# A twelve-stage decoder on one core: the delta-rule stage without its loop, and another order of work in the selective-scan stage

## The reference, cut to what matters

```
hs, gate = split(x @ Win.T)                       # 512 channels each
hs = silu(causal_conv4(hs) + bconv)
dt_in, Bm, Cm = split(hs @ Wx.T)                  # 128, 16, 16
dt = softplus(dt_in @ Wdt.T + bdt)
dA = exp(A * dt);  dBu = dt * Bm * hs             # per channel and state n of 16
h_t = dA_t * h_(t-1) + dBu_t;  y_t = sum_n h_t * C_t
out = ((y + hs * D) * silu(gate)) @ Wout.T
```

```
q, k, v = split(silu(causal_conv4(x @ Wqkv.T)));  z = x @ Wz.T
beta = sigmoid(x @ Wb.T);  g = -exp(A_log) * softplus(x @ Wa.T + dt_bias)
state = exp(g_t) * state
state = state + k_t (v_t - state k_t) * beta_t;   out_t = state q_t
result = (rmsnorm(out) * norm_w * silu(z)) @ Wout.T
```

## Time and profile before

| | |
|---|---|
| profiled execution | 4954.54 us |
| its span, first to last instruction | 4952.8 us |
| median of three runs | 4951.31 us |
| PE busy | 4182.5 us (84%) |
| DVE busy | 3232.5 us (65%) |
| ACT busy | 2130.0 us (43%) |
| POOL busy | 1507.2 us (30%) |
| scans of l2_attn | from 977.05 to 1516.1 us |
| steps of l3_attn | from 2326.7 to 4287.2 us |
| mean granted PE clock, share of full speed | 0.926 |
| instruction queues q8 and q14 | 464 packets, 7.60 MB; 127 packets, 1.04 MB |

### The profile page before, as it was taken

One profiled execution on the slowest core, in us unless ns is written; L12 is line 12 of the kernel. 1 busy time (PEld: TensorE's weight loads), 2 busy tenths in 40 slices (PEclk: granted clock), 3 DMA queues, 4 the chain that ended last, 5 costly groups with the idle time before them and its releaser, 6 DMA issues. The chain is left out here.

```text
span 4952.8 us, 145582 instructions
## 1 busy us (share of the span) xinstructions
PE 4182.5 (84%) x62052; PEld 2732.9 (55%) x62052; DVE 3232.5 (65%) x6011; ACT 2130.0 (43%) x3774; POOL 1507.2 (30%) x1609
## 2 busy tenths in 40 slices
PE   7626886677767887997999999999999999779999
PEld 6515654323324664444676767676766767545555
DVE  6797644688887777744677777777777777531111
ACT  3446443644444554323554555555555555321111
POOL 1001100188893220000343433333433333212222
PEclk9869887888899998998999999999999999789999
DMA  0000000133341001001000000000000000031111
GB/s 32 18 26 10 0 12 19 46 116 114 123 141 45 1 1 33 20 0 39 18 20 21 20 21 20 21 20 21 21 23 21 20 20 4 8 115 49 53 54 45
DMA packets 70627, 174.60 MB, mean 35 GB/s; under 512 B 14322, under 2 KB 27636, under 8 KB 67444
## 3 DMA queue, kind: packets, MB, share of 16 engines
q1 hardware_dynamic: 70036, 165.96, 10.6%
HBM read 163.04 MB, written 2.88 MB: 34 GB/s over the span
## 5 line engine op out<-in xcount | busy, mean ns | idle before, releaser
L2416 POOL TENSOR_TENSOR dn_eb<-dn_ee,dn_cc 128x512 f32<-128x512 f32 x64 | 66.7, 1042 | 1119.6 <-DVE dn_cc L2530 1119.6
L2956 DVE TENSOR_TENSOR moe_hh<-moe_si,moe_pu 128x512 f32<-128x512 f32 x104 | 71.5, 688 | 450.5 <-PE moe_pu L2845 444.2
L1667 POOL TENSOR_TENSOR ssm_ub<-ssm_dtu,ssm_bcn 128x512 f32<-128x512 f32 x256 | 319.6, 1269 | 31.9 <-DVE ssm_ph L1726 29.1
L2123 PE MATMUL dn_bA<-core_XT,dn_w 128*128 128x512 f32 x512 | 274.3, 661 | 59.6 <-issue 41.3
L2460 DVE SCALAR_TENSOR_TENSOR core_XN<-dn_bA,dn_w,core_XN 128x504 f32<-128x504 f32 (+2 forms) x384 | 280.8, 731 | 44.0 <-ACT core_XN L2297 24.0
L1628 ACT ACTIVATE ssm_da<-core_XN,ssm_al 128x504 f32<-128x504 f32 x256 | 173.9, 683 | 253.5 <-DVE ssm_ph L1726 156.6
L1565 PE MATMUL ssm_py<-ssm_hc,core_ident 128*128 128x512 f32 x352 | 201.7, 675 | 74.6 <-DVE ssm_hc L1730 44.4
L2908 POOL TENSOR_TENSOR moe_hw<-moe_hh,moe_cb 128x512 f32<-128x512 f32 x100 | 126.7, 1267 | 451.5 <-DVE moe_hh L2956 392.3
L2889 ACT ACTIVATE moe_si<-moe_pg 128x512 f32<-128x512 f32 x104 | 62.1, 597 | 466.1 <-PE moe_pg L2845 466.1
L1726 DVE TENSOR_TENSOR_SCAN ssm_ph<-ssm_da,ssm_ub 128x512 f32<-128x512 f32 x176 | 214.7, 1220 | 47.6 <-ACT ssm_da L1628 25.5
L2255 PE MATMUL dn_po<-dn_wo,dn_cT 128*128 128x256 f32 x1024 | 240.8, 389 | 1.1 <-ACT dn_cT L2357 1.1
(11 more groups left out here) (515 smaller groups left out, 10511.3 us busy)
## 6 DMA issues: line engine op xcount, KB each, us to landing
ssm_bcn<-ssm_bct SPq DMA_DIRECT2D x128, 512.0 KB, 3.6
dn_cb<-dn_cum SPq DMA_DIRECT2D x32, 512.0 KB, 8.0
dn_w<-in_dn_w SPq DMA_DIRECT2D x16, 776.0 KB, 4.9
moe_cb<-moe_rows SPq DMA_DIRECT2D x64, 192.0 KB, 2.8
moe_w<-in_moe_w SPq DMA_DIRECT2D x26, 384.0 KB, 9.9
moe_cb<-moe_rows SPq DMA_DIRECT2D x64, 128.0 KB, 3.0
dn_wo<-in_dn_w SPq DMA_DIRECT2D x16, 256.0 KB, 3.7
moe_cb<-moe_rows SPq DMA_DIRECT2D x64, 64.0 KB, 2.6
```

The lines of the kernel that those rows point to most:

```text
L1667: pool.tensor_tensor(ub[u % NUB][:, :], dtu[q % 2][:, c, :], bcn[i % NB][:, 0, :], ALU.mult).then_inc(ub_ready, 1)
L2123: mm = pe.matmul(bank[:, :], wp[:, kc, gi * P:(gi + 1) * P], g.XT[:, kc, q * CH:(q + 1) * CH], start=kc == 0, stop=kc == DC - 1)
```

## The change

In l3_attn the loops go. `schedule` now writes out all 66 steps for each engine, and SP's loads are written out for all 16 heads. All waits are for the running sum from the start of the stage; `settle` and `take_now`, which took the counts off again, are gone. Addresses that were worked out from the loop's counter become constants. The order of the instructions of each engine is the same as before.

In l2_attn the order is another. Four decay factors (units 20 to 23 of each chunk) are computed into a new SBUF tile `dx` ahead of silu in the job S, so the scans of these units read `dx` in place of `da`. The gate projections Z of chunk 0 and the D jobs 2 and 3 are not ahead of the first unit: the Z stand between units 3 and 12 (as "Y"). D 0 now comes before X 1. The dt and dtu of D 0 and D 1 are made by VectorE. TensorE's X waits for each silu block alone. `ub` has four slots in place of three, `hc` four in place of eight.

```diff
-    NB, NUB, NHC = 4, 3, 8
+    NB, NUB, NHC, NDX = 4, 4, 4, 4
+        dx = s.sb("dx", [P, NDX, CH])
...
-        ahead = [("H", 0), ("H", 1), ("H", 2), ("H", 3), ("S", 0), ("X", 0), ("X", 1), ("D", 0), ("D", 1), ("D", 2), ("D", 3),
-                 ("Z", 0), ("Z", 1), ("Z", 2), ("Z", 3)]
+        ahead = [("H", 0), ("H", 1), ("H", 2), ("H", 3), ("S", 0), ("X", 0), ("D", 0), ("X", 1), ("D", 1)]
+        AT.update({("Y", c): 3 + 3 * c for c in range(IC)})
...
+            if j[0] == "Y":
+                return None if q else (0, ("Z", j[1]))
...
+        silu_at = AT["S", 0]
+        apart = lambda u: 0 <= u % (IC * N) - silu_at < NDX
+        factor = lambda u: dx[:, u % (IC * N) - silu_at, :] if apart(u) else da[:, u % 2, :]
...
                     elif kind == "X":
-                        pe.wait_ge(hs_ready, IC * (q + 1))
                         for kc in range(IC):
+                            pe.wait_ge(hs_ready, IC * q + kc + 1)
...
+                def decay(u):
+                    k, n, cc = split(u)
+                    q, c = k // 2, k % 2 * 2 + cc
+                    act.activation(nb(factor(u))[:, :, 1:S], nb(dt[q % 2][:, c, :])[:, :, 1:S], ACT.Exp,
+                                   scale=al[:, n, c:c + 1]).then_inc(da_ready, 1)
...
                     elif kind == "S":
+                        if q:
+                            for n in range(NDX):
+                                decay((q - 1) * IC * N + silu_at + n)
                         act.preload_act_table_set("silu_and_others")
...
+                    if apart(u):
+                        return
                     if u >= 2:
-                        act.wait_ge(scan_done, u - 1)
+                        act.wait_ge(scan_done, u - 1 - (NDX if apart(u - 2) else 0))
+                    decay(u)
...
-                    if kind == "D":
+                    if kind == "D" and q * IC + c >= 2:
                         pool.wait_ge(sp_ready, q * IC + c + 1)
...
                         dve.tensor_scalar(mm0[:, c % 2, :], out, tap(K + 2, c), 0.0, ALU.add, ALU.max).then_inc(m_ready, 1)
+                        if q * IC + c < 2:
+                            dve.wait_ge(sp_ready, c + 1)
+                            dve.drain()
+                            dve.tensor_tensor(dt[q][:, c, :], mm0[:, c, :], sa[:, c, :], ALU.add).then_inc(dt_ready, 1)
+                            dve.drain()
+                            dve.tensor_tensor(dtu[q][:, c, :], dt[q][:, c, :], hs[q][:, c, :], ALU.mult).then_inc(dtu_ready, 1)
...
-                        dve.tensor_tensor_scan(ph[:, m % 2, :], da[:, u % 2, :], ub[u % NUB][:, :], 0.0, ALU.mult, ALU.add).then_inc(scan_done, 1)
+                        dve.tensor_tensor_scan(ph[:, m % 2, :], factor(u), ub[u % NUB][:, :], 0.0, ALU.mult, ALU.add).then_inc(scan_done, 1)
...
-        def schedule(eng, step):
-
-            step(0, 0)
-            step(1, 0)
-            settle(eng)
-            with eng.Fori(0, 7) as a8:
-                for k in range(8):
-                    step(k + 2, a8 * 2)
-                settle(eng)
-            for i in range(58, NSTEP + 2):
-                step(i, 0)
-            settle(eng)
+        def schedule(step):
+
+            for i in range(NSTEP + 2):
+                step(i)
...
-                with nc.sync.Fori(1, NKH // 2) as kh2:
-                    for u in range(2):
-                        row = a["dn_w"][bass.ds(kh2 * 2 + u, 1), :, :]
-                        load_w(u, row)
-                        load_cb(u, kh2 * 2 + u)
-                        load_wo(u, row)
+                for kh in range(NKH):
+                    row = a["dn_w"][kh:kh + 1, :, :]
+                    if kh:
+                        load_w(kh % 2, row)
+                    load_cb(kh % 2, kh)
+                    load_wo(kh % 2, row)
```

More of the change, by code:

```diff
@@ L1447, in jobs_at @@
                 return q + 1, j
-        order = [(0, j) for j in ahead if j[0] != "S" and j not in later.values()]
+        order = [(0, j) for j in ahead if j[0] != "S"]
         for q in range(NQ):
@@ L1476, in schedule @@
             for j in ahead:
-                if j not in later.values():
-                    job(0, j)
+                job(0, j)
             for u in range(NU):
@@ L1662, in unit @@
                     q, c, i = k // 2, k % 2 * 2 + cc, u // 2
+                    if u < 2:
+                        pool.wait_ge(dtu_ready, u + 1)
                     if cc == 0:
@@ L1681, in _ @@
                     dve.memset(nb(da[:, k, :])[:, :, 0:1], 0.0)
+                for k in range(NDX):
+                    dve.memset(nb(dx[:, k, :])[:, :, 0:1], 0.0)
                 dve.drain().then_inc(a_exp, 1)
@@ L2182, in level_x, with step @@
                     mm.then_inc(px_ready, 1)
-                def step(i, _):
+                def step(i):
                     new, mid, old = i < NSTEP, 0 < i <= NSTEP, i >= 2
@@ L2278, in _ @@
                 pe.matmul(bB[:, :], lt[:, :], gg[:, :, :].rearrange("p t h -> p (t h)"), start=True, stop=True).then_inc(cum_ready, 1)
-                schedule(nc.tensor, step)
+                schedule(step)
             @block.scalar
@@ L2384, in _ @@
                 decays(0)
-                schedule(nc.scalar, step)
+                schedule(step)
             @block.gpsimd
@@ L2402, in decays, with step @@
                     pool.tensor_scalar(gm[i % 2][:, :, :], gm[i % 2][:, :, :], 0.0, None, ALU.min).then_inc(gm_ready, 1)
-                def step(i, kh0):
+                def step(i):
                     new, old = i < NSTEP, i >= 2
@@ L2430, in step @@
                             pool.tensor_tensor(halves(mb[i % 2][:, l - 1, :]), BD[:, :, :], bcm(small[:, 1 + l, :], NS), ALU.mult).then_inc(mb_ready, 1)
-                decays(0, 0)
-                decays(1, 0)
-                schedule(nc.gpsimd, step)
+                decays(0)
+                decays(1)
+                schedule(step)
             @block.vector
@@ L2483, in update, with step @@
                     last.then_inc(upd_ready, 1)
-                def step(i, kh0):
+                def step(i):
                     new, mid, old = i < NSTEP, 0 < i <= NSTEP, i >= 2
                     m, o = i - 1, i - 2
-                    kh, q = i // NCH + kh0, i % NCH
+                    kh, q = i // NCH, i % NCH
                     if old:
@@ L2529, in step @@
                         dve.drain()
-                        dve.tensor_tensor(two(cc), bt[:, q * TPC:(q + 1) * TPC, bass.ds(kh * 2, 2)], bc(rk[:, :], 2),
+                        dve.tensor_tensor(two(cc), bt[:, q * TPC:(q + 1) * TPC, kh * 2:kh * 2 + 2], bc(rk[:, :], 2),
                                           ALU.mult).then_inc(c_ready, 1)
@@ L2555, in step @@
                             dve.sem_inc(wo_free, 1)
-                schedule(nc.vector, step)
+                schedule(step)
 def l3_xattn(nc, g, a):
```

39 lines of the change are left out of this document (13 added, 26 removed).

## The result

| | before | after |
|---|---|---|
| median of four runs each | 4951.62 us (4946.84 to 4957.85) | 4913.57 us (4912.58 to 4914.41) |
| ratio to before | | 0.9922, 95% interval 0.9905 to 0.994 |
| profiled execution, its span | 4954.54, 4952.8 us | 4914.12, 4912.3 us |

The kernel is 38 us faster where 67 were forecast, and its time lies 4.6 us above the upper end of the range. The forecast was wrong. The table splits the 40.5 us between the spans. It is worked out from the starts of one instruction for each step (`dn_eb` of GpSimd, as in the earlier trace rows) less 28.5 us, and from the starts of the scans.

The account below looks back on a forecast made before the run. TensorE bounds l3_attn; VectorE and GpSimd share the bound in l2_attn. 56 + 12.1 - 7 + 3.7 - 1 + 3 = 66.8, taken as 67 us off 4951.3: 4884 us, range 4863 to 4909 us.

Parts of the forecast that it names:

- The loop's edges: In l3_attn, removing the loop ends waits of 41.3 us and the slow projections behind them: 56 us (45 to 58).
- The stalls beside the loads stay: In l3_attn, TensorE's waits for late instruction packets beside loads, about 27 us, remain: no cost, up to 10 us either way.
- more late packets: Rival, chance 0.08: in l3_attn new packet edges fall inside more load bursts, twice the 27 us of stalls: 4911 us.
- Four decay factors ahead of silu: In l2_attn, ScalarE makes the factors of units 20 to 23 before job S, shrinking VectorE's waits: 12.1 us gained.
- the price of dx in SBUF: In l2_attn, sixteen scans with two SBUF inputs lengthen beside GpSimd, which has slack: 7 us lost (0 to 17).
- dx loses what it gains: Rival, chance 0.16: dx's upper price or Z jobs leave l2_attn gaining nothing to losing 5 us: 4895 to 4901 us.
- A fourth `ub`: In l2_attn, another slot lets GpSimd run further ahead, shrinking VectorE's 12.9 us of waits by 3 (0 to 5).
- The start of l2_attn: At l2_attn's start, X 0 begins earlier and D 0 precedes X 1, so the first scan comes 3.7 us earlier.

Follow-up runs that it names:

- e1: The kernel after the change, with l2_attn as before it, so only l3_attn is changed: 4918.77 us, ratio to before 0.9929.
- e4: The kernel after with 128 already-met waits put ahead of l3_attn in TensorE's list, moving its later instructions by half a packet: 4910.6 us, ratio to before 0.9914.
- e3: The kernel after with SP's loads in l3_attn spread in time (second half of dn_cb, then dn_w, issued later): 4871.7 us, ratio to before 0.9831.
- e2: The kernel after the change, with l3_attn and its loop as before, so only l2_attn is changed: 4945.03 us, ratio to before 0.9983.
- e6: As e3 (loads spread), but with no dx: all decay factors are made in da: 4874.8 us, ratio to before 0.9836.
- e7: As e3 (loads spread), but with two dx slots in place of four: 4860.27 us, ratio to before 0.9813.
- e8: As e3 (loads spread, four dx), but with three ub slots in place of four: 4872.39 us, ratio to before 0.9832.

## Why the prediction was wrong

**The loop's edges: right.** 53.1 us of 56, with no "issue" wait of over 3 us on the projection, and a step of 28.50 where 36.82 was.

**"The stalls beside the loads stay": this step failed.** I read from the earlier trace rows that a packet was late beside the loads, and from the earlier trace rows that straight code needs as many of them, and costed the change at nothing with 10 us to either side. The rate was right (368 packets in the stage after, 381 before, 451 against 464 on the page). But the rate isn't what costs. What costs is that no packet comes until 5 to 9 us behind the burst's issue, so it matters how much of its instructions TensorE still holds when the burst starts. The loop, by restarting the packets each turn, had kept that good at nine heads of 14; in straight code it drifts through worse places, and longer stalls brought the half clock at seven heads in place of three. The term measured +19.5 us, nearly twice the bound I gave it. e1 shows it without l2_attn, e4 moves it with the positions, e3 takes it away. The sum has luck in it too: 20.5 us in e2 and 27.2 before for the same loop, 43.4 to 50.1 in the four kernels of straight code with the burst.

It was the rival "more late packets", at 4911 us with a chance of 0.08, 2.6 us from the result. Its mechanism was the right one, and new positions were its reason; the load steps came to 46.8 us where it had 54. It should have had more: the prediction itself named position as what the stalls hang on, and the change moves every position.

The rule on instruction fetching that the prediction weighed (the Trainium skill, "Runtime: NRT & Kernel Launch", section Instruction fetch mechanics: crossing a block is mostly hidden) doesn't hold beside a burst: 4.66 us in one place, 46.8 us in all with the half clock. It holds once the burst is spread: 2.4 us in all.

**"Four decay factors ahead of silu" and "the price of dx in SBUF": the waits went, the gain didn't.** The first term's reason was right, VectorE's 16.3 us of waits for ScalarE are gone but for 1.2; by chunks the gain was 1.7, 0.9 and 0.4 us and a loss of 1.8, where 2.7, 3.96, 3.96 and 1.5 were forecast (less the price of `dx`). In e2 and e4, with the same text, chunks 1 and 2 gained 3.6 and 1.4: there VectorE waits less at units 27 and 29. So how much is lost depends on the build too. The price on VectorE was right as well: 27.6 - 19.4 = 8.2 us for my 7. What failed is the other side of it, of which I said that GpSimd has slack there. These are GpSimd's two largest groups of the stage (960 to 1520 us: count, busy us, mean ns, idle before), in e3 with four `dx`, then in e6 with none:

```profile
L1685 POOL TENSOR_TENSOR ssm_ub<-ssm_dtu,ssm_bcn 128x512 f32<-128x512 f32 x256 | 324.4, 1292 | 308.5 <-DMA ssm_bcn<-ssm_bct 306.1 <-issue 0.8 <-DVE ssm_hb L1747 0.6
L1674 POOL TENSOR_TENSOR ssm_hp<-ssm_hb,ssm_bcn 128x512 f32<-128x512 f32 x80 | 108.3, 1354 | 52.0 <-DVE ssm_hb L1747 52.0
```

```profile
L1684 POOL TENSOR_TENSOR ssm_ub<-ssm_dtu,ssm_bcn 128x512 f32<-128x512 f32 x256 | 318.0, 1268 | 308.5 <-DMA ssm_bcn<-ssm_bct 306.0 <-issue 0.8 <-DVE ssm_hb L1746 0.6
L1673 POOL TENSOR_TENSOR ssm_hp<-ssm_hb,ssm_bcn 128x512 f32<-128x512 f32 x80 | 101.3, 1267 | 65.2 <-DVE ssm_hb L1746 65.0
```

GpSimd lost 6.4 + 7.0 = 13.4 us for the same instructions. And VectorE then waits for what comes from there or from behind it: +5.3 us of waits "<- issue" and +1.0 for `ub`. From 16.3 + 1.0 (`hb` waits for ScalarE 9.1, now 8.1) less 8.2, 5.3, 1.0 and the 1.2 at unit 24 of chunk 0 some 2 us are left; the stretch shows 1.2. That was the rival "dx loses what it gains", 0.16. The new waits "<- issue" (1.15 us at unit 24 in chunks 1 to 3, 2.6 at unit 22 of chunk 0) end 0.09 us behind the unit's `ub`, as shown above. At unit 24 that `ub` is one that a `dx` scan lengthened to 2.18 us: GpSimd's loss is handed on there. With no `dx` the waits "<- issue" are 8.0 us in all (e6) and with two 8.6 (e7), so the rise belongs to the four. Why the `ub` of unit 22 starts so late in chunk 0 stays open.

Here the rule of the Trainium skill ("SBUF — State Buffer", section SBUF: two separate sides, on engine ports: an exclusive lock, the loser blocks fully) was the better guide: the prediction worked out 19 us of loss for GpSimd by it, and from the rows none that costs; 13.4 were measured.

**"A fourth `ub`": mis-sized.** 3 us forecast, 0 measured (e8). The waits at units 42, 45 and 48 are 1.5, 1.2 and 2.6 us with either number, so GpSimd was behind by its rate and not for want of a slot.

**The start of l2_attn: right,** 4.4 us for 3.7, with B and C copied at 965.45 (965.7 forecast).

The sum: 67 forecast; less 19.5 for the load steps, 2.9 for the edges and 5.9 for the scans with their slots; 0.7 more at the start. That makes 39.4 us; the profiled executions have 4954.54 - 4914.12 = 40.4, so some 1 us lies elsewhere.

## What to carry to other kernels

Here the instruction packets (q8) and the data (q1) went through the same 16 DMA engines. When straight code replaces a loop, or any edit shifts the instructions, look at every big burst (1.8 MB did harm here, 0.79 MB did not) for a missing instruction packet and for "issue" waits some 6 to 10 us behind it, and spread the burst over the engine's work: here that was worth more (42 us) than the removal of the loop (34). And when an operand moves from PSUM to SBUF on VectorE beside a busy GpSimd, charge both engines, and move as few as cover the wait.

## What the hardware showed that I had not expected

- With a burst of 1.8 MB 7.1 to 10.4 us lay between two of TensorE's instruction packets, and the next came 4.9 to 8.7 us behind the burst's issue. With 0.79 MB it came 3.4 to 4.7 us behind it, and TensorE's longest "issue" wait on the small matmuls was 1.0 us.
- A stall of 1.22 us was followed by 8 us at half clock in one step and by none in another, and their excess was 4.9 and 1.9 us.
- At one place the wait behind the loop's jump grew from 6.61 to 8.81 us when 768 KB were in flight beside it in place of 256.
- A scan of 1.21 us took 2.22 us and GpSimd's instruction of 1.27 us took 2.18 us in the same microseconds.
- The same text of l2_attn gave stretches of 534.1 and 537.9 us in different builds, mostly from VectorE's waits for ScalarE at units 27 and 29 (8.1 us in the kernel after, 4.3 in e2). Why isn't known.
